# Last of 128 row tiles fetched row by row from the SP queue instead of by an indirect gather, and transposed first of its pair

## What is computed

```python
e = jnp.stack([tbl_0[ids[:, 0]], ..., tbl_31[ids[:, 31]]], axis=1)   # 512 x 32 x 256
dots = jnp.einsum('bnd,bmd->bnm', e, e)
z = dots[:, iu, ju]                                  # 496 pairs with i < j
h = jnp.concatenate([z, dense_ctx], axis=1)          # 512 x 512
h = jnp.maximum(h @ W_top1 + b_top1, 0.0)            # 512 x 512
h = jnp.maximum(h @ W_top2 + b_top2, 0.0)            # 512 x 256
y = h @ W_top3                                       # 512 x 1
```

## Time and profile before

| | |
|---|---|
| median of 3 runs | 211.35 us (211.13 to 211.7) |
| the profiled execution's own time | 212.17 us |
| its span, first to last instruction | 210.4 us |
| mean granted TensorE clock | 0.87 |
| PE busy | 152.6 us, 73% |
| POOL busy | 122.7 us, 58% |
| DVE, ACT busy | 76.4 and 64.3 us |
| DMA, mean over the span | 89 GB/s |

### The profile page before, as it was taken

How to read it: one execution, slowest core, us unless ns; L and a number is a source line. 1 busy time by engine, 2 the same in 40 slices (tenths; PEclk the granted TensorE clock), 3 DMA queues, 4 the chain that set the end, 5 groups by cost and what they waited for, 6 DMA issues and landing times.

```text
span 210.4 us, 2889 instructions
## 1 busy us (share of the span) xinstructions
PE 152.6 (73%) x1022; PEld 136.9 (65%) x1022; DVE 76.4 (36%) x240; ACT 64.3 (31%) x194; POOL 122.7 (58%) x135
## 2 busy tenths in 40 slices
PE   0558177376858999676497979596598988666995
PEld 0358067276758898565386868585486878555894
DVE  0110160437162153734153153634162263616321
ACT  2011141335050261524133251515143251515241
POOL 4777475657577466757575657757575675751010
PEclk9996958969696799998569999978569999979799
DMA  1494233223323223323232332323232332321000
GB/s 44 131 352 148 75 99 104 62 88 98 101 80 101 76 79 90 108 75 100 75 103 75 100 100 76 101 76 102 72 108 74 97 101 76 100 75 50 3 0 0
DMA packets 7759, 18.80 MB, mean 89 GB/s; under 512 B 2593, under 2 KB 3489, under 8 KB 7618
## 3 DMA queue, kind: packets, MB, share of 16 engines
q0 software_dynamic: 6144, 16.79, 27.5%
q1 hardware_dynamic: 1602, 1.84, 2.8%
HBM read 18.62 MB, written 0.00 MB: 89 GB/s over the span
## 4 chain that ended last, share of the span: by engine, by line
PE 56%; issue 13%; another core or an unknown queue 11%; DVE 9%; ACT 7%; DMA 2%; POOL 1%; DVEq 0%; ACTq 0%
PE gram_ps L341 29%; PE xt_ps L320 12%; PE mlp_ps L379 5%; PE mlp_ps L387 4%; ACT z L190 4%; DVE slots L232 3%; DVE xt L213 2%; ACT xt L213 2%; PE mlp_ps L366 2%; DVE z L190 2%; DMA rows<-in_table,row_number 1%; PE mlp_ps L396 1%; DVE slots L242 1%; PE xt_ps L379 1%
## 5 line engine op out<-in xcount | busy, mean ns | idle before, releaser
L201 POOL DMA_INDIRECT rows<-in_table,row_number x128 | 121.7, 951 | 68.0 <-issue 33.0
L341 PE MATMUL gram_ps<-xt 128*128 128x128 f32 x504 | 83.9, 320 | 43.3 <-ACT xt L213 17.5
L341 PEld LDWEIGHTS gram_ps<-xt 128*128 128x128 f32 x504 | 75.0, 228 | 50.8 <-ACT xt L213 20.0
L213 DVE COPY xt<-xt_ps 128x512 f32<-128x512 f32 x32 | 22.1, 692 | 97.6 <-PE xt_ps L320 45.2
L320 PE MATMUL xt_ps<-identity,rows 128*128 128x128 f32 x256 | 48.1, 317 | 10.5 <-DMA rows<-in_table,row_number 10.5
L320 PEld LDWEIGHTS xt_ps<-identity,rows 128*128 128x128 f32 x256 | 36.4, 165 | 13.2 <-issue 7.0
L213 ACT COPY xt<-xt_ps 128x512 f32<-128x512 f32 x31 | 18.1, 585 | 57.1 <-remote 20.1
L190 DVE COPY z<-slots 32x32 f32<-32x32 f32 x142 | 31.6, 222 | 2.4
L190 ACT COPY z<-slots 32x32 f32<-32x32 f32 x111 | 27.2, 245 | 11.3 <-DVE slots L242 6.9
L232 ACT COPY slots<-gram_ps 32x256 f32<-32x256 f32 (+1 forms) x32 | 11.5, 361 | 45.6 <-PE gram_ps L341 18.2
L232 DVE COPY slots<-gram_ps 32x256 f32<-32x256 f32 (+1 forms) x32 | 13.1, 410 | 8.0 <-remote 2.8
(11 more groups left out here) (26 smaller groups left out, 23.0 us busy)
## 6 DMA issues: line engine op xcount, KB each, us to landing
rows<-in_table,row_number POOLq DMA_INDIRECT x128
w1z_sb<-in_w1z SPq DMA_DIRECT2D x1, 1024.0 KB
w_sb<-in_w SPq DMA_DIRECT2D x1, 512.0 KB
ids_sb<-in_ids SPq DMA_DIRECT2D x1, 64.5 KB, 1.8
identity<-in_eye SPq DMA_DIRECT2D x1, 64.0 KB, 2.1
upper_sb<-in_takes_upper SPq DMA_DIRECT2D x1, 64.0 KB
ctx_sb<-in_ctx_t SPq DMA_DIRECT2D x1, 32.0 KB
w1c_sb<-in_w1c SPq DMA_DIRECT2D x1, 32.0 KB
```

The source lines that it names most:

```text
L201: nc.gpsimd.indirect_dma_start(rows[:, n % RING, :], None, table, bass.IndirectOffsetOnAxis(ap=row_number[:, n:n + 1], axis=0),).then_inc( ...
L213: copy(xt[:, p % XT_RING], xt_ps[p % 2][:]).then_inc(xt_ready[p % 2], 1)
L341: done = nc.tensor.matmul(product_ps(n), x, x, start=(k == 0), stop=(k == KD - 1))
```

## The change

POOL gathers tiles 0 to 126. Behind its eight loads of constants SP waits for all row numbers, and then, 128 times, loads one row number from SBUF into a register and issues a DMA of that row (1 KB, as two runs of 512 B) to one partition of a new buffer, `last_rows`. All of them count on one semaphore, 16 each. PE's transposes of tile 127 wait for 2048 and read `last_rows`. In the last pair tile 127 is now transposed, copied and multiplied before 126: 127 goes to bank 1 and is still copied by ACT, 126 goes to bank 0 and is still copied by DVE.

```diff
@@ buffers, semaphores, PSUM place
+        last_rows = sbuf("last_rows", [P, KD, P + 4])
+        last_rows_landed = sem("last_rows_landed")
         def tile_ps(n):
-            return xt_ps[0][:, 0] if n == TILES - 1 else xt_ps[n // 2 % 2][:, n % 2]
+            return xt_ps[0][:, 0] if n == TILES - 2 else xt_ps[n // 2 % 2][:, n % 2]
@@ SP
             sp.dma_start(w3_sb[:], w3).then_inc(w3_loaded, 16)
+            sp.wait_ge(numbered, 2)
+            for r in range(P):
+                row = sp.value_load(row_number[r:r + 1, TILES - 1:TILES], min_val=0, max_val=table.shape[0] - 1)
+                sp.dma_start(last_rows[r:r + 1, :, 0:P], table[bass.ds(row, 1), :].rearrange("r (k d) -> r k d", k=KD)
+                             ).then_inc(last_rows_landed, 16)
             sp.wait_ge(y_ready, LAST + 1)
@@ POOL
-            for n in range(TILES):
+            for n in range(TILES - 1):
@@ copy_last
-            engine.wait_ge(transposed, LAST_PAIR + 1 + i)
+            engine.wait_ge(transposed, LAST_PAIR + 2 - i)
@@ PE: transpose
-                pe.wait_ge(rows_landed[n % RING], 16 * (n // RING + 1))
+                if n == TILES - 1:
+                    pe.wait_ge(last_rows_landed, 16 * P)
+                else:
+                    pe.wait_ge(rows_landed[n % RING], 16 * (n // RING + 1))
                 for k in range(KD):
-                    done = nc.tensor.transpose(tile_ps(n)[:, k, :], rows[:, n % RING, k * P:(k + 1) * P], identity[:])
+                    held = last_rows[:, k, 0:P] if n == TILES - 1 else rows[:, n % RING, k * P:(k + 1) * P]
+                    done = nc.tensor.transpose(tile_ps(n)[:, k, :], held, identity[:])
@@ PE: last_transposes
                 pe.wait_ge(xt_ready[1], LAST_PAIR // 2)
+                transpose(TILES - 1).then_inc(transposed, 1)
+
+                pe.wait_ge(xt_ready[0], LAST_PAIR // 2 + 1)
                 transpose(TILES - 2).then_inc(transposed, 1)
-
-                pe.wait_ge(xt_ready[0], LAST_PAIR // 2 + 1)
-                transpose(TILES - 1).then_inc(transposed, 1)
@@ PE: last_gram
                 pe.wait_ge(y_ready, LAST)
+                pe.wait_ge(last_xt_ready[1], 1)
+                product(TILES - 1)
                 pe.wait_ge(last_xt_ready[0], 1)
-                product(TILES - 2)
-                pe.wait_ge(last_xt_ready[1], 1)
-                product(TILES - 1).then_inc(gram_ready, 1)
+                product(TILES - 2).then_inc(gram_ready, 1)
```

## The result

The changed kernel takes 305.32 us (median, 303.26 to 308.52), the kernel before 211.52 us in the same comparison: ratio 1.4366, interval 1.4186 to 1.4546. The prediction was 211.5 us, with 214.0 as the upper end of its range. The rival "SP is late" is what happened. The execution that was profiled is the longest of the four, 308.52 us.

The account below looks back on a forecast made before the run. The prediction took PE with its waits for copies as the bound, POOL in its shadow. Gather 0, SP 0, traffic 0 and swap 0.1 us on the 211.35 us median gave 211.5 us, range 210.3 to 214.0.

Parts of the forecast that it names:

- SP is late: PE's wait before tile 127: every turn above 1.43 us moves the end by 128 times the excess; chance 0.19.
- the value of a turn: SP's loop: load, check, arithmetic and issue take 1.1 us a row, last row landed at 154.6 us, 42 us early.
- The break-even and the price: SP's loop: free up to 1.43 us a row; beyond that the end moves by 128 times the excess.
- The odds: Whole kernel: no change beyond the swap 0.62; within 0.3% 0.60, slower 0.30, faster 0.10; late SP 0.19.
- The gather, 0: POOL's end: dropping the last gather is worth 0, as tile 127 lies ready 4.6 us early; uncovered, at most 1.25 us.
- The traffic, 0: DMA queues: 128 rows of 1 KB, 0.13 MB at 0.9 GB/s beside 91 GB/s, leave gathers room; worth 0.
- new waits for gathered rows: PE during SP's loop: row DMAs hold up gathers, 0.5 us in two or three places, 212.5 to 213; chance 0.05.
- The swap, +0.1: Last pair: ACT's copy of the now-first tile ends later than DVE's did, so products end 0.09 us later.

Follow-up runs that it names:

- eight-a-load kernel with the old order: Changed kernel with eight row numbers per register load, no bounds check, and tile 126 before 127 in the last pair: 225.88 us against 212.2 us for the kernel before.
- the fixed rows: Changed kernel with its 128 row DMAs reading fixed table rows, no register loads or checks: 226.72 us, ratio 1.0523 to the kernel before, where that took 216.06 us.
- eight a load with the check: Changed kernel with eight row numbers per register load, bounds check on, tile 127 before 126: 235.94 us (single run), the kernel before 212.2 us.

## Why the prediction was wrong

**The step that failed** is the value of a turn. That the load "is nearer to the smallest steps of an engine than to a DMA" put it at 0.28 us, check and arithmetic at about as much, the issue at 0.54, in sum 1.1 us. Measured in the quiet stretches of the changed kernel: load 0.74, check 0.3, arithmetic and address move 0.07 with 0.08 of gaps, issue 0.63 and 0.05 behind it: 1.87 us, and 2.16 on average beside the working engines of the slow place. The load alone was off by a factor of 2.6 and makes 0.46 of the missing 0.77 us. The Trainium skill, DMA: Bandwidth & Descriptors, Latency and other measured facts, has about 600 ns as the floor of a `tensor_load`. The traces agree in size, with medians of 0.73 to 0.74 us, and not as a strict floor: the very first load of the changed kernel in the fast place took 0.47. That one number would not have been enough: with the 0.54 us of issue it still gave 1.14 us, under the limit of 1.43.

**The break-even and the price were right.** 1.43 us a turn as the limit, and 128 times the excess behind it: 211.35 + 128 x (2.16 - 1.43) = 305 us, measured 305.32. That it fits to the microsecond is luck: the 2.16 is from the profiled execution, which took 308.52, and the formula has no term for the tail. With one the sum closes there: 212.17 + (289.38 - 196.44) + 3.3 for the tail at a low clock is 308.4. In the fast place PE wants the last pair at about 165 us, which leaves about 1.2 us a turn: 1.58, without the check, is over it and waited for, and 0.89, with eight numbers a load, is under it and not waited for.

**The odds were wrong too.** The range of the turn was given as 0.54 to 2.64 us with the limit at 1.43, not far from the middle. Bounds that lie on both sides of a limit as these did do not carry four chances in five for one side; the text spoke of 0.9 us as room, though check, arithmetic and load had each to be paid from it 128 times.

**The gather, 0:** right in the slow place by the traces (no late wait for gathered rows), with a time that cannot tell it from 1.25 us; not right in the fast one (0.26% less).

**The traffic, 0:** wrong in the slow place. Bytes and DMA share were weighed, and they are indeed small, but 128 issued row DMAs cost some 10 to 14 us there (226.72 against 216.06, 225.88 against 212.2). The recorded rival for this, new waits for gathered rows, is not how it happens: PE waits 8.0 us for them in the changed kernel and waited 10.5 before. What the traces show instead is more pauses of the whole core and a lower clock (last section). In the changed kernel the idle 80 us hide this: PE ended pair 62 at 208.41 us, where it had ended at 196.65, so this time would probably have been lost even with the rows there in time.

**The swap, +0.1:** right in the slow place's trace (+0.10), mis-sized in the fast place, 0.31 us in the traces, and too small for any run's time.

## What to carry to other kernels

A register load followed by the DMA that needs it is a serial chain on its sequencer; count it as load + check + issue, here 1.87 us, and multiply by the number of turns before asking whether anything covers it. Loading several registers with one instruction (0.04 us for each further one) and dropping the bounds check took the turn to 0.89 us (1.17 in the slow place). And a queue that is idle is no proof that its use is free: in the slow place 128 small DMAs, long done when they were wanted, cost 5%, and so no version tried that fetches the last tile by rows beats the kernel before. The eight-a-load kernel with the old order was not run in the fast place.

## What the runs showed of the hardware

The same program takes 180.4 to 180.8 us on some chips, most runs with a mean granted clock of 0.95 to 1.0, and 211 to 216 us on others, with 0.85 to 0.93. That moves the bound: on the former POOL's 1.25 us steps set the pace, on the latter PE and what it waits for.

The clock is not the whole difference. PE is busy for 152.6 us of the first trace and for 138.0 us of the fast one; the other half of the 31.8 us between the spans is idle time. The two traces of this one program run alike for some 20 us, and then the engines of the slow one stand: PE, DVE and ACT until 25.3, and POOL ends the gather that it had begun and goes on at 25.57. PE's and DVE's rows, and windows with the columns of the earlier trace rows, of the kernel before in the slow place:

```profile
20.93 0.60 PE L320 MATMUL xt_ps<-identity,rows 128*128 128x128 f32 x4
26.08 1.55 PE L341 MATMUL gram_ps<-xt 128*128 128x128 f32 x8 [4.56 <-DVE xt L213]
25.34 0.69 DVE L213 COPY xt<-xt_ps 128x512 f32<-128x512 f32 x1 [9.40 <-remote]
21.60:25.30 3.70, 0.00 (x0) 0.00 (x0) 0.00 (x0) 0.00 (x0) 1.06 (x2) 1.00 0.26 80
26.70:33.40 6.70, 5.52 (x26) 5.11 (x26) 3.18 (x12) 2.88 (x9) 5.05 (x6) 0.50 0.35 100
```

and in the fast place:

```profile
20.95 0.60 PE L320 MATMUL xt_ps<-identity,rows 128*128 128x128 f32 x4
21.39 1.06 PE L341 MATMUL gram_ps<-xt 128*128 128x128 f32 x8
20.26 0.69 DVE L213 COPY xt<-xt_ps 128x512 f32<-128x512 f32 x1 [3.99 <-PE xt_ps L320]
21.60:25.30 3.70, 1.70 (x15) 1.47 (x14) 3.42 (x12) 2.59 (x9) 2.79 (x4) 1.00 0.35 102
```

DVE copies pair 4 at 25.34 us, though its transposes ended at 20.20 (19.33 and 0.87 us); in the fast place it copies at 20.26. The clock still stands at its upper level in the pause, and falls to the lower one behind it. So here the pause comes first and the clock follows. I counted the stretches of more than 1.4 us between 14 us and the last pair in which none of PE, DVE, ACT and POOL starts an instruction. The eleven traces of the fast place have none. In the slow place the four kernels without row DMAs have 4 to 6, of 10 to 15 us in all. Three kernels with them (the changed one, the fixed rows, eight a load in the old order) have 9 or 10, of 21 to 24 us; the fourth (eight a load with the check) has only 5, of 12 us.

In the slow place SP's small instructions come in stretches in which each takes about 0.7 us (the maxima of the changed kernel's source lines: 699 ns for the assertion, 710 for a register operation), and not in the fast place (37 and 179 ns). Such a stretch lies across a pause: of 15 to 23.2 us in the changed kernel, in whose last 3.5 us (from 19.73) no other engine starts anything. Once the other engines stand for good, from about 209 us on, SP's turns are nearly even. What makes the pauses is not shown. Nor is it shown why row DMAs bring more of them, or how that goes with their number.

With all engines idle PE's clock stayed at the lower level for the whole wait, 73 us, and 3 us of the tail are its price.
